# Causal attention in units of two heads, with the score maxima and the exponentials of different heads in one interleaved sequence

## What is computed

```python
q, k, v = heads(q), heads(k), heads(v)                  # 16 heads
q_lat = q @ q2l_w.T + q2l_b                              # 32 latent features per head
k_lat = k @ kv2l_w.T + kv2l_b
v_lat = v @ kv2l_w.T + kv2l_b
...                                                      # rotary embedding of q_lat and k_lat
q_for_k = q_lat @ wqk_w.T + wqk_b
att = jnp.einsum('bhql,bhkl->bhqk', q_for_k, k_lat) * L ** (-0.5)
att = jnp.where(causal[None, None], att, -jnp.inf)
att = jax.nn.softmax(att, axis=-1)
y_lat = jnp.einsum('bhqk,bhkl->bhql', att, v_lat)
y = y_lat @ l2o_w.T + l2o_b
return y.transpose(0, 2, 1, 3).reshape(B, T, C) @ cproj_w.T + cproj_b
```

## Time and profile before

| | |
|---|---|
| time of the kernel, median of 3 runs | 4242.39 us (4240.14 to 4256.25) |
| the profiled execution: time, span | 4273.73 us, 4272.0 us |
| mean granted TensorE clock, share of full | 0.934 |
| busy share: PE, DVE, ACT, POOL | 87%, 52%, 32%, 21% |

### The profile page before, as it was taken

The page is one execution under the profiler, slowest core; times in us unless marked ns, Lnnn a source line. Parts: engine busy times, 40 slices in busy tenths (PEclk is TensorE's granted clock), DMA queues, the critical chain, the costliest instruction groups (busy, mean ns, idle before and its releaser), DMA issues. The chain is left out here.

```text
span 4272.0 us, 83914 instructions
## 1 busy us (share of the span) xinstructions
PE 3732.4 (87%) x34672; PEld 2248.0 (53%) x34672; DVE 2221.5 (52%) x4555; ACT 1376.0 (32%) x2456; POOL 884.0 (21%) x1248
## 2 busy tenths in 40 slices
PE   6988898899798889889979888988987988898898
PEld 4863354465486335456548543535655854353565
DVE  5755434554575544364467554445436745443643
ACT  4422222432443231243144313224315421322531
POOL 2620101120262010122026201012203610101310
PEclk9989999989999999998999989999899988999989
DMA  2001000010000100001000010000000001000010
GB/s 89 3 13 51 21 19 1 25 39 28 28 3 13 51 21 19 1 25 39 28 28 4 12 51 21 19 1 25 39 28 28 4 12 51 21 19 1 25 39 30
DMA packets 10941, 104.25 MB, mean 24 GB/s; under 512 B 1148, under 2 KB 5552, under 8 KB 6192
## 3 DMA queue, kind: packets, MB, share of 16 engines
q1 hardware_dynamic: 10544, 98.69, 6.1%
HBM read 97.64 MB, written 1.05 MB: 23 GB/s over the span
## 5 line engine op out<-in xcount | busy, mean ns | idle before, releaser
L89 PE MATMUL psum<-ident_bf 128*128 128x512 bf16 x2012 | 546.7, 410 | 147.3 <-DVE l_attn_peak L913 56.5
L89 PEld LDWEIGHTS psum<-ident_bf 128*128 128x128 bf16 x2012 | 198.4, 105 | 405.9 <-issue 154.0
L496 DVE TENSOR_TENSOR l_ffn_hidden<-l_ffn_silu,psum 128x512 f32<-128x512 f32 (+2 forms) x176 | 120.9, 687 | 319.8 <-ACT l_ffn_silu L435 319.8
L435 ACT ACTIVATE l_ffn_silu<-psum 128x512 f32<-128x512 f32 (+1 forms) x208 | 124.2, 597 | 472.4 <-PE psum L404 418.8
L95 PEld LDWEIGHTS psum<-streamed_weights,l_ffn_hidden 128*128 128x128 f32 (+1 forms) x1664 | 215.2, 191 | 113.9 <-issue 103.2
L151 POOL TENSOR_TENSOR norm_rstd<-norm_var,minus_half 128x2 f32<-128x2 f32 x104 | 75.4, 725 | 893.6 <-DVE norm_var L164 893.2
L2824 PE MATMUL psum<-l_attn_xx,l_attn_part 64*64 64x64 f32 x5120 | 223.6, 223 | 28.5 <-DVE l_attn_xx L3237 19.3
L913 DVE TENSOR_REDUCE l_attn_peak<-psum 128x4 f32<-128x2048 f32 (+3 forms) x128 | 185.9, 1487 | 99.3 <-PE psum L808 99.2
L3032 ACT ACTIVATE l_attn_ax<-psum 128x256 f32<-128x256 f32 x320 | 122.5, 384 | 343.4 <-PE psum L2824 333.6
L95 PE MATMUL psum<-streamed_weights,l_ffn_hidden 128*128 128x128 f32 (+1 forms) x1664 | 223.4, 277 | 8.4 <-DVE l_ffn_hidden L493 5.0
L2824 PEld LDWEIGHTS psum<-l_attn_xx,l_attn_part 64*64 64x64 f32 x5120 | 196.9, 136 | 53.1 <-DVE l_attn_xx L3237 23.7
(11 more groups left out here) (542 smaller groups left out, 7871.2 us busy)
## 6 DMA issues: line engine op xcount, KB each, us to landing
streamed_weights<-pack_l_ffn SPq DMA_DIRECT2D x4, 5284.0 KB, 15.3
streamed_weights<-pack_l_ffn SPq DMA_DIRECT2D x4, 3972.0 KB, 12.7
streamed_weights<-pack_l_attn SPq DMA_DIRECT2D x5, 2848.5 KB, 9.8
streamed_weights<-pack_l_xattn SPq DMA_DIRECT2D x4, 2496.0 KB, 8.9
streamed_weights<-pack_l_ffn SPq DMA_DIRECT2D x4, 2192.0 KB, 8.0
streamed_weights<-pack_l_xattn SPq DMA_DIRECT2D x4, 2048.0 KB, 7.4
streamed_weights<-pack_l_ffn SPq DMA_DIRECT2D x4, 1923.0 KB, 8.1
streamed_weights<-pack_l_attn SPq DMA_DIRECT2D x4, 1107.5 KB, 5.0
```

The costliest lines, as they stand in the source:

```text
L89: pe.matmul(self.bank(bank), self.ident_bf[:, :], self.ident_bf[:, :].unsqueeze(1).to_broadcast([P, NT, P]), start=True, stop=True)
L435: act.activation(silu[0:r, n % 2, :], m.bank(n % 2)[0:r], ACT.Silu).then_inc(silu_ready, 1)
L496: dve.tensor_tensor(hidden[0:r, n % 2, :], silu[0:r, n % 2, :], m.bank(2 + n % 2)[0:r], ALU.mult).then_inc(hidden_ready, 1)
```

## The change

The two phases become one sequence of items. An item is a unit of scores or of exponentials for **two heads** (h = 0: heads 0 and 1 of a group, h = 1: heads 2 and 3), or a turn. `plan` lists the items step by step: in steps 0 to 3 only the score items of units 0 to 3; from step 4 on the exponential unit t-4 (LAG = 4) together with score unit t, in the order exponentials of heads 0/1, scores of heads 2/3, scores of heads 0/1, exponentials of heads 2/3; in steps 12 to 15 exponentials alone. Item n uses banks 2(n mod 3) and the next one, three pairs in rotation, and waits until item n-3 has been read. Banks 6 and 7 (NEAR, FAR) hold the mix of queries 0-255 and 256-511, sums in one half of the columns and values in the other. At the end of each step from 5 on, TensorE mixes unit t-5. A unit of exponentials is now: keys 0-255 for the near queries; keys 0-255 for the far queries; keys 256-511 for the far queries. VectorE divides each half as soon as it is complete.

The diff, cut (removed lines of the old functions are mostly left out; they stand in full above):

```diff
-    G, R, W, SLOTS = 4, 4, 32, 3
+    G, R, W, SLOTS, LAG = 4, 4, 32, 3, 4
+    HALF = T // 2
+    NEAR, FAR = 6, 7
     quad = lambda r: slice(W * r, W * r + W)
-    steps = []
-    for g in range(G):
-        for i in reversed(range(NT)):
-            steps.append(("scores", g, i))
-            if g > 0 and i == 2:
-                steps.append(("turn", g - 1, 0))
-    parts = [[(0, 0)], [(1, 0), (3, 3 * P)], [(2, 0)]]
-    units = [(g, part) for g in range(G) for part in parts]
-    diagonals = [sum(len(part) for _, part in units[0:u + 1]) for u in range(len(units))]
+    heads = lambda h: range(2 * h, 2 * h + 2)
+    pair = lambda h: slice(2 * h, 2 * h + 2)
+    tiles = [[(3, 0)], [(2, 0)], [(1, 0), (0, 2 * P)]]
+    pieces = [[(0, 0, HALF, 0), (1, P, HALF, HALF)], [(0, HALF, T, 0), (1, HALF, T, HALF)],
+              [(2, HALF, T, 0), (3, 3 * P, T, HALF)]]
+    N1 = N2 = 3 * G
+    plan, items = [], []
+    for t in range(N2 + LAG):
+        now = []
+        scores = [("scores", t, h) for h in (range(2) if t < LAG else (1, 0))] if t < N1 else []
+        exps = [("exps", t - LAG, h) for h in range(2)] if t >= LAG else []
+        now = exps[:1] + scores + exps[1:]
+        if t % 3 == 0 and 1 <= t // 3 <= G:
+            now.append(("turn", t // 3 - 1, 0))
+        plan.append([len(items) + n for n in range(len(now))])
+        items += now
...
+        bank = lambda n, r=0: 2 * (n % 3) + r % 2
+        banks = lambda n: slice(2 * (n % 3), 2 * (n % 3) + 2)
...
+                def scores(n, a, h):
+                    g = a // 3
+                    for at, (i, c) in enumerate(tiles[a % 3]):
+                        for r in heads(h):
+                            pe.matmul(m.psum[:, bank(n, r), c:c + (i + 1) * P], q_of(g)[quad(r), i * P:(i + 1) * P],
+                                      k_of(g)[quad(r), 0:(i + 1) * P], start=at == 0, stop=False, skip_group_check=True)
+                    for i, c in tiles[a % 3]:
+                        for r in heads(h):
+                            ins = pe.matmul(m.psum[:, bank(n, r), c + i * P:c + (i + 1) * P], m.ident_bf[:, :],
+                                            m.later_bf[:, :], start=False, stop=True, skip_group_check=True)
+                    ins.then_inc(scores_ready, 1)
+
+                def exps(n, b, h):
+                    g = b // 3
+                    for at, (j, lo, hi, c) in enumerate(pieces[b % 3]):
+                        for r in heads(h):
+                            pe.matmul(m.psum[:, bank(n, r), c:c + hi - lo], k_of(g)[quad(r), j * P:(j + 1) * P],
+                                      q_of(g)[quad(r), lo:hi], start=at == 0, stop=False, skip_group_check=True)
+                    pe.wait_ge(shiftT_ready, g + 1)
+                    for j, lo, hi, c in pieces[b % 3]:
+                        for r in heads(h):
+                            ins = pe.matmul(m.psum[:, bank(n, r), c:c + hi - lo], one_bf[W * r:W * r + 2, :],
+                                            shiftT[W * r:W * r + 2, g, lo:hi], start=False, stop=True, skip_group_check=True)
+                    ins.then_inc(shifted_psum, 1)
...
+                def mix(b):
+                    g, u = divmod(b, 3)
+                    for h in range(2):
+                        pe.wait_ge(exps_ready, copied[b, h])
+                        pe.wait_ge(causal, masked[b, h])
+                    if not shared and g >= 1 and u < 2:
+                        pe.wait_ge(mixed_ready, 2 * g - 1 + u)
+                    to, base = (NEAR, 0) if u == 0 else (FAR, HALF)
+                    for at, (j, lo, hi, c) in enumerate(pieces[u]):
+                        for of_sums in (True, False):
+                            shifted = HALF * of_sums - base
                             for r in range(R):
-                                lhsT = v[:, j, head_of(g, r), :] if n == 0 else ones_of(g)
-                                ins = pe.matmul(m.psum[quad(r), bank + n, lo:hi], lhsT,
-                                                prob[:, u % SLOTS, r, c + lo - j * P:c + hi - j * P],
-                                                start=j == 0 and (g == 0 or not shared), stop=True, skip_group_check=True)
-                            if n == 1 and u == U - 1:
-                                ins.then_inc(group_summed, 1)
-                        return ins
-
-                    if not shared and g == G - 1 and u % len(parts) == 1:
-                        pe.wait_ge(mixed_ready, G - 1)
-                        products(u - 1, 0, 0, HALF, T, far_bank(g))
-                    for j, c in part:
-                        if not shared and g < G - 1:
-                            ins = products(u, j, c, j * P, T, mix_bank(g))
+                                ins = pe.matmul(m.psum[quad(r), to, lo + shifted:hi + shifted],
+                                                ones_of(g) if of_sums else v[:, j, head_of(g, r), :],
+                                                prob[:, b % SLOTS, r, c:c + hi - lo],
+                                                start=of_sums and at == 0 and u < 2 and (g == 0 or not shared), stop=True,
+                                                skip_group_check=True)
+                    ins.then_inc(unit_mixed, 1)
...
+                pe.wait_ge(cleared, 2)
+                for t, now in enumerate(plan):
+                    for n in now:
+                        kind, a, h = items[n]
+                        if n >= 3:
+                            if t < LAG:
+                                m.warm(pe, 2, FAR)
+                            wait_consumed(n - 3)
+                        if kind == "scores":
+                            scores(n, a, h)
+                        elif kind == "exps":
+                            exps(n, a, h)
                         else:
-                            if j * P < HALF:
-                                ins = products(u, j, c, j * P, HALF, mix_bank(g))
-                            if shared or j > 0:
-                                ins = products(u, j, c, max(HALF, j * P), T, far_bank(g))
-                    ins.then_inc(group_mixed, 1)
-
-                for u in range(U + 2):
-                    if u < U:
-                        shifted(u)
-                    if u == 0:
-                        wait_consumed(pe, len(steps) - 2)
-                        turn(G - 1, 4)
-                    if u >= 2:
-                        mix(u - 2)
+                            turn(n, a)
+                    if t > LAG:
+                        mix(t - LAG - 1)
+                mix(N2 - 1)
...
+                    elif kind == "exps":
+                        act.wait_ge(shifted_psum, copied[a, h])
+                        if a >= SLOTS:
+                            act.wait_ge(unit_mixed, a - SLOTS + 1)
+                        act.activation(prob[:, a % SLOTS, pair(h), 0:width(a % 3)], m.psum[:, banks(n), 0:width(a % 3)],
+                                       ACT.Exp).then_inc(exps_ready, 1)
...
+                def divide(g, far):
+                    cols = slice(HALF * far, HALF * far + HALF)
+                    at = (0 if shared else 2 * g) + far
+                    dve.wait_ge(unit_mixed, 3 * g + 2 * far + 1)
+                    dve.reciprocal(inverse[:, cols], m.psum[:, NEAR + far, HALF:T]).then_inc(inverse_ready, 1)
+                    dve.wait_ge(inverse_ready, at + 1)
+                    dve.tensor_tensor(mixed[:, group_of(g), cols], m.psum[:, NEAR + far, 0:HALF], inverse[:, cols],
                                       ALU.mult).then_inc(mixed_ready, 1)
...
+                done = 0
+                for t, now in enumerate(plan):
+                    for n in now:
+                        kind, a, h = items[n]
+                        if kind != "scores":
+                            continue
+                        done += 1
+                        dve.wait_ge(scores_ready, done)
+                        for i, c in tiles[a % 3]:
+                            dve.tensor_reduce(peak[:, a // 3, i, pair(h)], m.psum[:, banks(n), c:c + (i + 1) * P], AX, ALU.max,
+                                              negate=True).then_inc(peak_ready, 1)
+                    if t < N1 and t % 3 == 2:
+                        spread(t // 3)
+                    if not shared and t > LAG:
+                        g, u = divmod(t - LAG - 1, 3)
+                        if u != 1 and t < len(plan) - 1:
+                            divide(g, u // 2)
+                if shared:
+                    divide(G - 1, 0)
+                divide(G - 1, 1)```

How TensorE's program moves. In layer 1's phase 1, one group of heads before; a row is a line, the operation, output and inputs, its width, and how many stand in a row (x4: one for each head):

```order
L805 MATMUL psum<-l_attn_k,l_attn_q 128x512 x4
L808 MATMUL psum<-later_bf,ident_bf 128x128 x4
L89 MATMUL psum<-ident_bf 128x512
L805 MATMUL psum<-l_attn_k,l_attn_q 128x384 x4
```

161 lines of the change are left out of this document (46 added, 115 removed).

## The result

The changed kernel is slower, by 0.8%. Its median is 4289.74 us (4261.2 to 4319.89, 13 runs) against 4245.27 us (4238.85 to 4278.22, 13 runs) for the kernel before on the same chip; the ratio is 1.0077, with a 95% interval of 1.0048 to 1.0107. The prediction, 4227 with a range of 4170 to 4275, is missed on the slow side.

The account below looks back on a forecast made before the run. TensorE was the bound, busy 87% though useful work filled neither phase; its 78.6 us list less 5.3 overlap plus waits gave 75.2, with half clock and end 83.7 and 79.6, 15 us less in all: 4227, range 4170 to 4275.

Parts of the forecast that it names:

- For layer 1 I keep the 8 us after the start: Start of layer 1's attentions: half clock for 8 us as before, 7.8 busy us losing 3.9 us.
- the rival "the clock": Two-head steps leave half clock for 3.4 us three times more an attention: 41 us, 4268; a fourth 4281; chance 0.10.
- The added wait: Start of each attention: TensorE waits for GpSimd's two memsets before its first scores, 1.1 us that nothing covers.
- 75.2: TensorE's time an attention at full clock in us: list of 73.3 after overlap, plus the added waits.
- score items: TensorE's two-head scores with masks and shape change: 1.29, 1.08 and 1.20 us, sum 3.57, x8 = 28.6 us an attention.
- the waits for the first exponentials and the last mix: TensorE waits 0.5 us for the first turn's copy and ScalarE's table, 0.3 us for last exponentials and GpSimd.
- the later stretch at half: In both layers' attentions, one stretch of 3.4 us at half clock after the start, costing 1.7 us.
- The overlap: Scores start beside exponentials in other rows, six rows ahead, at 12 places: 12 x 0.44 = 5.3 us saved an attention.
- The rival "nothing overlaps": Matmuls keep program order, so the attention loses 4 us of the saving: 32 us, 4259; chance 0.10.
- "everything overlaps": Scores of heads 2/3 vanish under the exponentials, 12.2 instead of 5.3 us: 55 us more saved, 4172; chance 0.20.
- TensorE waited neither for ScalarE nor for VectorE: Forecast hid both under TensorE; a rival had exponential waits of 0.5 us a step, 64 us, 4291, chance 0.12.
- the profiled execution lies 31 us above the median: Conversion taken from the kernel before: 4259 for the profiled execution becomes 4227 against a median of 4242.4.

Follow-up runs that it names:

- experiment 2: Changed kernel with 14 extra items of one, two or four heads ahead of layer 1's attention, executed once each: 4377.73, 4385.57 and 4291.57 us.
- before_prewarm: Kernel before with 28 idle matmuls at the end of layer 1's block ahead of the attention: 4243.19 us, ratio 0.9982.
- no_start_idle: Changed kernel with 28 idle matmuls ahead of layer 1's attention and the memset wait moved to the first exponentials in both layers: 4193.43 us, ratio 0.9874.
- experiments 5 and 7: 5 is no_start_idle, 4193.43 us; 7 is the change in layer 2's attention alone, layer 1 as in the kernel before: 4287.76 us.
- experiments 6 to 8: 6: changed kernel, 16 idle matmuls at layer 1's start, 4286.11 us; 7: change in layer 2 alone, 4287.76; 8: both with memset wait moved, 4214.69 and 4230.46.

## Why the prediction was wrong

**The step that failed is the clock** at the start of layer 1's attentions, in two sentences of the prediction. "For layer 1 I keep the 8 us after the start" took the recovery of four-head work over to two-head work. With two-head work the half clock reaches 24.8 to 52.6 us into the attention (windows of the changed kernel; experiment 2 shows why). The term was 3.9 us in the forecast and is up to 26. And the rival "the clock" was given 0.10 and put aside by the row from 110 to 260 us, where the clock was granted. That row shows a clock that is kept, at a place where it was full; it says nothing about one that has to be won back. Nor is it a case of 64 rows: L2824's pieces alternate between both halves of the rows, and they are 51 of the 142 busy us there. The two-head steps keep full clock as well, in every attention that got past its start with it. The rival's shape was wrong too: stretches of 3.4 us, a few more of them, where the cost is one stretch of 20 to 55 us, until idle matmuls with a turn, or the mixes, end it.

**The added wait was priced at 1.1 us** and measured so (0.42 to 1.53 us idle). Its real price is that it can lose the clock at a start, and two-head work does not bring it back: 9.5 to 17 us an attention, in 12 of 32.

**At full clock the forecast was too cautious.** From the first scores to the last mix's end it is 71.6 us (649.61 to 721.26), with 1.1 for the memsets 72.7, against 75.2. Named terms that were off: score items 1.27, 1.06 and 1.08 instead of 1.29, 1.08 and 1.20 (8 x 0.16 = 1.3 us), and the waits for the first exponentials and the last mix (0.5 and 0.3 us forecast, 0.0 idle measured). Outside this sum, the later stretch at half did not come (1.7 us forecast, 0 measured). The overlap was sized nearly right: scores start 0.55 us after exponentials of 256+128 columns, where I gave 0.6, and eight of the twelve places are worth 3.0 us, where 0.44 each makes 3.5. The rival "nothing overlaps" is out; "everything overlaps" is out too. The Trainium skill ("TensorE: Matmul & The Clock Gate", Part 3: Packing small matmuls) says that matmuls start and end in program order; for matmuls in different rows these traces disagree, 0.55 us against the 0.92 us that the order would take, and the measurement decides. TensorE waited neither for ScalarE nor for VectorE. The fair comparison of the two structures is before_prewarm with no_start_idle: 50 us between the medians, 46 by the ratios, at the same care for the start. The attentions alone gain 4 x (8.2 + 7.5) = 63 us; outside them no_start_idle has 425 us at half clock where before_prewarm has 388, which takes up to 19 back.

**The sum of it, and luck.** By the profiled executions alone the forecast looks right: 4259 us forecast, 4262.67 measured, from 4273.73. That is luck. Layer 2's attentions gained 26 us where 4 x 1.65 was forecast, layer 1's lost 34 where a gain of 4 x 2.1 was, and the rest of the program, forecast as unchanged, is 19 us shorter in spite of the eight later starts. It has 379 us at half clock instead of 471, which is not the change's doing as far as experiments 5 and 7 show how it varies.

**From the profiled execution to the median.** The prediction took over that the profiled execution lies 31 us above the median. For the changed kernel it lies 27 us below. The record has the mean granted clock of each execution: 0.936 of full in the profiled one, 0.930 in the median one, 0.922 in the longest. As time at half clock that is some 546, 600 and 674 us, so the clock can account for up to 27 and 64 us, and the executions are 27 and 57 us longer. So the executions differ by their time at half clock. That it lies in attentions that fall (each takes up to 17 us more, four in layer 2 up to 68) is argued from experiments 6 to 8, since the other executions left no trace.

## What to carry to other kernels

Before a step is cut into pieces that use fewer rows of the array, look at the granted clock at its start, not in its middle. In this kernel full clock was kept by such pieces and not regained by them, so the idle time ahead (1.5 and 6.5 us) had to be filled or moved. A wait for something that is needed only later can cost more than its length when it is the first thing in such a phase; moving it to where the thing is needed is an edit of a few lines. And where passes of the same instructions differ in one trace, a median needs more than the one profiled execution to be explained.

## What the runs showed of the hardware that was not expected

- Half clock with TensorE busy 27.00 of 27.00 us (two-head steps) and 23.78 of 24.00 (two heads alone); up to 78.5 us in one stretch. Four heads of the same matmuls: back in 4.4 to 4.7 us, 4 of 4. Idle matmuls of the whole array: back in 4.4 us in the first pass, and full at the first scores in 4 of 4.
- The same two-head steps at full clock keep it for 71.5 to 76.9 us, in every attention that started with it and had not lost it within 3.1 us of its first scores.
- A start at full clock behind 1.5 us of idle time fell in 12 of 32 cases, between 0.9 and 3.1 us after the first scores; behind 0.4 us in none of 36. Which of the 32 it was is not explained; that edits in layer 1 alone moved layer 2 from 0 of 4 to 4 of 4 speaks for the place of the start in time, which no run varied by itself.
- A matmul in other rows starts while earlier ones are still queued: 0.55 us after the first of twelve rows that take 0.92 us to the next item where nothing may overlap (661.16 to 662.08).
